# Attention with routed experts on one core: biases loaded as rows, gates and shared product ahead of the keys' second half, the scale product with one tensor from SBUF

## What is computed

```python
q = (x @ Wq + bq).reshape(b, h, t, dh)            # 16 heads of 128; a plain reshape, no transpose
k = (x @ Wk + bk).reshape(b, t, h, dh).transpose(0, 2, 3, 1)
v = (x @ Wv + bv).reshape(b, t, h, dh).transpose(0, 2, 1, 3)
logits = jnp.einsum('bhtd,bhds->bhts', q, k) * scale          # causal mask, softmax
out = jnp.einsum('bhts,bhsd->bhtd', weights, v).transpose(0, 2, 1, 3).reshape(b, t, h * dh) @ Wo + bo
...
shared = jax.nn.silu(g_s) * y_s @ w_shared_down               # g_s, y_s halves of x @ w_shared_up
scores = jax.nn.sigmoid(x_flat @ w_gate)                      # 64 experts, 6 of them for each token
# each expert takes its first 128 tokens: silu(x @ g) * (x @ v) @ w_down, added with normalised scores
```

## Time and profile before

| | |
|---|---|
| median of 3 runs | 1931.96 us (1929.65 to 1937.21) |
| the profiled execution | 1928.67 us |
| its span on the core | 1926.9 us |
| mean granted PE clock | 0.964 of full speed |
| PE busy | 1666.5 us (86%) |
| DVE busy | 1536.8 us (80%) |
| ACT busy | 1083.2 us (56%) |
| POOL busy | 1154.6 us (60%) |
| DMA, mean | 127 GB/s |

### The profile page before, as it was taken

The page is one execution under the profiler, slowest core; times in us unless marked ns, Lnnn a source line. Parts: engine busy times, 40 slices in busy tenths (PEclk is TensorE's granted clock), DMA queues, the critical chain, the costliest instruction groups (busy, mean ns, idle before and its releaser), DMA issues. The chain is left out here.

```text
span 1926.9 us, 49610 instructions
## 1 busy us (share of the span) xinstructions
PE 1666.5 (86%) x19088; PEld 1296.6 (67%) x19088; DVE 1536.8 (80%) x3189; ACT 1083.2 (56%) x2347; POOL 1154.6 (60%) x1004
## 2 busy tenths in 40 slices
PE   1589989999899999999876789998998989999996
PEld 1466777777667777777655767766676776677674
DVE  4888878888788888888854458988988898988885
ACT  0556566666566666656552236655665655566564
POOL 0156667777677777777660027666666666766653
PEclk8799999999999999999997589999999999999999
DMA  9266656565655555545557648777878778777865
GB/s 346 95 136 118 120 114 123 122 114 104 124 90 95 92 99 99 93 87 94 118 95 201 193 112 140 124 133 132 144 129 142 130 143 135 130 123 127 149 119 103
DMA packets 692723, 245.04 MB, mean 127 GB/s; under 512 B 643584, under 2 KB 680785, under 8 KB 691600
## 3 DMA queue, kind: packets, MB, share of 16 engines
q1 hardware_dynamic: 657344, 197.80, 56.1%
q0 software_dynamic: 18432, 33.64, 7.1%
q10 hardware_dynamic: 16720, 10.51, 1.9%
HBM read 57.11 MB, written 50.46 MB: 56 GB/s over the span
## 5 line engine op out<-in xcount | busy, mean ns | idle before, releaser
L476 POOL TENSOR_TENSOR prob<-prob 128x128 f16<-128x128 f32 (+7 forms) x512 | 662.5, 1297 | 626.9 <-ACT prob L856 620.2
L849 ACT ACTIVATE prob<-prob,nmax 128x128 f32<-128x128 f32 (+7 forms) x512 | 397.0, 775 | 644.3 <-DVE prob L1291 631.5
L687 PE MATMUL ps_s<-kT,qT 128*128 128x512 f16 (+3 forms) x2304 | 457.6, 326 | 7.3 <-DVE prob L1291 3.6
L702 PE MATMUL ps_o<-probT,vh 128*128 128x256 f16 (+1 forms) x3840 | 425.3, 264 | 6.5 <-DMA probT<-prob 5.8
L1291 DVE TENSOR_SCALAR_CACHE_REDUCE prob<-ps_s,neg_scale 128x128 f32<-128x128 f32 (+7 forms) x512 | 409.8, 808 | 2.9 <-PE ps_s L689 2.0
L702 PEld LDWEIGHTS ps_o<-probT,vh 128*128 128x128 f16 x3840 | 367.4, 99 | 50.7 <-issue 7.5
L856 ACT CAST prob<-prob 128x128 f16<-128x128 f32 (+7 forms) x512 | 341.5, 667 | 2.2
L687 PEld LDWEIGHTS ps_s<-kT,qT 128*128 128x128 f16 x2304 | 199.5, 98 | 147.0 <-issue 13.1
L716 PE MATMUL ps_y<-wo,oT 128*128 128x256 f16 x1536 | 210.8, 273 | 85.6 <-DVE oT L1306 58.5
L579 PE MATMUL ps_t<-xT,wq 128*128 128x64 f16 x6144 | 202.5, 195 | 61.8 <-DVE z L1193 22.9
L579 PEld LDWEIGHTS ps_t<-xT,wq 128*128 128x128 f16 x6144 | 193.3, 99 | 73.5 <-issue 33.2
(11 more groups left out here) (173 smaller groups left out, 1759.4 us busy)
## 6 DMA issues: line engine op xcount, KB each, us to landing
dispatched<-zeros SPq DMA_DIRECT2D x16, 512.0 KB, 14.8
probT<-prob SPq DMA_TRANSPOSE x512
ex<-dispatched SPq DMA_DIRECT2D x16, 512.0 KB, 4.5
expert_out<-eo ACTq DMA_DIRECT2D x16, 512.0 KB, 4.0
eup<-in_L_ffn_w_up_dram SPq DMA_DIRECT2D x64, 64.0 KB, 2.1
dispatched<-xn,slot_idx POOLq DMA_INDIRECT x192
xn_columns<-xnth SPq DMA_DIRECT2D x24, 128.0 KB
got<-expert_out,slot_idx POOLq DMA_INDIRECT x192
```

Of the source, the lines that this page charges most:

```text
L476: pool.tensor_tensor(low_cols(j), prob_cols(j).rearrange("p (r k) -> p r k", k=P), high_cols(j), ALU.subtract).then_inc(p_low, 1)
L687: pe.matmul(s_cols(j, lo, hi), qT[:, u, a, j * P:(j + 1) * P], kT[:, u, c, lo:hi], start=(n == 0), stop=(n == 2 and hi < w))
L702: mm = pe.matmul(ps_o[:, lo:2 * P], vh[:, u, a, r * D:(r + 1) * D], probT[:, PT_AT[c] + 2 * r + s, lo:], start=(r + n == 0), stop=(r == 2 ...
L849: nc.scalar.activation(prob_cols(j), prob_cols(j), ACT.Exp, bias=nmax[:, j:j + 1], scale=-1.0, accum_out=rsum[:, i % 2, j:j + 1]).then_inc ...
```

## The change

It does three things. (1) The biases are loaded by SP, behind the first batch of x, as 48 rows of 128 into `bias_rows`, which POOL has cleared; PE turns them with one transpose into `ps_o`, and DVE builds `bvB` from there and copies `bqT` and `bkT`. ACT issues no loads at the start. (2) In the heads PE does `gates` and `shared_down` ahead of `project_k(i + 1, 1)`; ACT does `copy_gates` ahead of `high_k(i, 1)`; DVE does `take_logits` and `add_shared` ahead of `low_k(i, 1)`, moves `low_q(i, 1)` behind `block_max(i, 1)`, and `top_indices` and `choose` behind `full_q`; POOL does its three additions for the mask one or two blocks later. (3) `yscale` is computed by a scalar product whose scalar is `out_scale`, with a minimum accumulated into `yleast`, which nothing reads.

```diff
-        bvT = psb("bvT", [P, H])
+        bias_rows = psb("bias_rows", [P, D])
...
             sp.dma_start(resid[:, 0:TB, :], x_v[:, 0:TB, :]).then_inc(x_in[0], 16)
+            sp.wait_ge(bias_zero, 1)
+            for n, b in enumerate((bq, bk, bv)):
+                sp.dma_start(bias_rows[n * H:(n + 1) * H, :], b.rearrange("(m d) -> m d", d=D)).then_inc(bias_in, 16)
...
         def _(pool):
+            pool.memset(bias_rows[:], 0.0).then_inc(bias_zero, 1)
...
-                        if odd_part(i) >= 0 and j in (1, 2, 3):
-                            add_chosen(odd_part(i), j - 1)
+                        if odd_part(i) >= 0 and j == 2:
+                            add_chosen(odd_part(i), 0)
+                        if odd_part(i) >= 0 and j == 3:
+                            add_chosen(odd_part(i), 1)
+                            add_chosen(odd_part(i), 2)
...
             pe.wait_ge(const_ready, 5)
+            pe.wait_ge(bias_in, 48)
+            pe.transpose(ps_o[:, 0:P], bias_rows[:], ident[:]).then_inc(bias_done, 1)
...
                     scores(i, 7)
-                    if more:
-                        project_k(i + 1, 1)
                     if even_part(i) >= 0:
                         gates(i, even_part(i))
                     if odd_part(i) >= 0:
                         shared_down(i, odd_part(i))
+                    if more:
+                        project_k(i + 1, 1)
...
-            act.dma_start(bqT[:], bq.rearrange("(m d) -> d m", d=D)).then_inc(bias_in, 16)
-            act.dma_start(bkT[:], bk.rearrange("(m d) -> d m", d=D)).then_inc(bias_in, 16)
-            act.dma_start(bvT[:], bv.rearrange("(m d) -> d m", d=D)).then_inc(bias_in, 16)
...
-                    high_k(i, 1)
                     if odd_part(i) >= 0:
                         copy_gates(odd_part(i))
+                    high_k(i, 1)
...
-            dve.wait_ge(bias_in, 48)
-            V.tensor_copy(bvB[:], bvT[:].unsqueeze(2).to_broadcast([P, H, P])).then_inc(bias_ready, 1)
+            dve.wait_ge(bias_done, 1)
+            V.tensor_copy(bvB[:], ps_o[:, 2 * H:3 * H].unsqueeze(2).to_broadcast([P, H, P])).then_inc(bias_ready, 1)
+            V.tensor_copy(bqT[:], ps_o[:, 0:H]).then_inc(bias_taken, 1)
+            V.tensor_copy(bkT[:], ps_o[:, H:2 * H]).then_inc(bias_taken, 1)
+            dve.wait_ge(bias_taken, 2)
...
-                V.tensor_tensor(yscale[:], rinv[:], out_scale[:].to_broadcast([P, TB]), ALU.mult).then_inc(r_step, 1)
+                V.tensor_scalar(yscale[:], rinv[:], out_scale[:], None, ALU.mult, ALU.min, accum_out=yleast[:]).then_inc(r_step, 1)
...
                     block_max(i, 0)
-                    low_q(i, 1)
                     mix_at(0)
-                    low_k(i, 1)
                     if odd >= 0:
                         take_logits(odd)
                     if late >= 0:
                         add_shared(late, NC * (i - 1))
+                    low_k(i, 1)
...
                     block_max(i, 1)
+                    low_q(i, 1)
...
-                    if odd >= 0:
-                        top_indices(odd)
-                        choose(odd)
...
                         full_q(i + 1, 1)
+                    if odd >= 0:
+                        top_indices(odd)
+                        choose(odd)
```

More of the change, by code:

```diff
@@ L155, in causal_attention_with_moe @@
         x_in = [sem(f"x_in{n}") for n in range(3)]
+        bias_zero = sem("bias_zero")
         bias_in = sem("bias_in")
+        bias_done = sem("bias_done")
+        bias_taken = sem("bias_taken")
         w_in = sem("w_in")
@@ L264, in causal_attention_with_moe @@
         yscale = sb("yscale", [P, TB])
+        yleast = sb("yleast", [P, 1])
         pro = ExitStack()
```

## The result

The changed kernel takes 1921.8 us in the median (1915.7 to 1923.0, 5 runs) where the kernel before, on the same chip, takes 1933.8 (1929.7 to 1937.2): ratio 0.9931, 95% interval 0.9908 to 0.9955. It is faster, but by a third of what was forecast (1897.0), and it lies above the range (1875 to 1918). The profiled execution of after took 1922.98 us, its span is 1921.2, 5.7 shorter than before's 1926.9.

What follows compares the result with a forecast made beforehand. The DVE and ACT chain was taken as the bound, with PE ahead of it. -19.6 - 30.8 - 1.8 + 14.0 + 4.2 - 0.9 = -34.9 from 1928.67 gave 1893.8, with the runs' median 3.3 higher 1897; range 1875 to 1918.

Steps and rivals of the forecast that it cites:

- the late heads: 27 heads, 35 to 62 without 47: faster `yscale`, less the moved `low_q`, starts `qf` 1.14 us earlier each; -30.8 us.
- the turns: Turns of batch, heads 15, 31, 47: SP's queue behind `prob` 7 sets xT and hides the delay; 0 us.
- the even heads: 16 early heads: `low_q` fits a gap and only holds up the indirect DMA, 0.26 us each; +4.2 us.
- the odd heads: 14 early heads with routing: moved `low_q` is in the chain, block maximum 2 comes 1.0 us later; +14.0 us.
- the start: Before head 0: bias loads leave ACT's queue, square root 10.4 us earlier, `bvB` 21.2 earlier; -19.6 us in all.
- Rival (d): Start gives nothing, as the loads or PE at its half clock hold it: -15.3 us, 1917; chance 0.07.
- the product doesn't wait: Late heads' `yscale`, beside POOL's `prob` 7: 0.27 us against 2.19 before, -1.9 us.
- rival (c): The new product still waits for the rest of POOL's `prob` 7, with `low_q` on top: 1951, slower; chance 0.09.
- two SBUF inputs wait, one does not: DVE beside POOL's product: two-input `yscale` waits, 2.09 us; the reciprocal with one SBUF input takes 0.19.
- PE's waits at nothing: In the heads: DVE and ACT form the chain, PE runs ahead, so each edit is costed by that chain alone.
- (a): The move of `low_q` is absorbed by missed slack, heads 0 to 32 stay: -53.1 us, 1879; chance 0.17.
- (b): PE sets the early heads, so its 44.5 us of waits come back: -97.6 us, 1834; chance 0.05.

Runs made afterwards that it cites:

- filled: The changed kernel plus 24 unread small products on TensorE in every even early head where it waits for the query slices: 1908.7 us, ratio 0.9876.
- reorder_only: The kernel before with the reordering alone, without the bias part and the scale product: 1973.8 us, ratio 1.0204.
- low_q_late: The kernel before with bias part, scale product and, of the reordering, only `low_q`'s second half moved behind block maximum 1: 1918.0 us, ratio 0.9918.
- together: The changed kernel with `low_q`'s second half back, slot indices behind the query slices, and turn loads one transposition earlier: 1839.0 us, ratio 0.9524.

## Why the prediction was right or wrong

Of the 29.2 us between the forecast sum (-34.9) and the measured one (-5.7) the late heads are 18.9, the turns 8.7 and the even heads 8.5; the odd heads came out 6.7 better.

**Right: the start.** -19.6 forecast, -20.4 in the trace, -22.7 (ratio 0.9888) in the run of the part alone. `bvB` was forecast at 21.7 with 2.2 us and stood at 21.23 with 2.28; the table load did go ahead of the wait. Rival (d) fell.

**Right: the product doesn't wait, and rival (c) fell, but for another reason than I gave.** 0.22 us against the 0.27 I took. But the step "two SBUF inputs wait, one does not" is wrong as a rule: the plain form with one SBUF input takes 2.10 us, to the end of POOL's product. The row I leant on, the reciprocal, could not tell the forms apart, and `neg_mean`, which could have, I gave to the rival with 0.09. Had the product been written in the plainer way, (c) would have come true.

**Wrong: the size of the late heads, -30.8 for -11.9.** The mechanism held up to `qf`, which came 0.96 us earlier (forecast 1.14), with the keys waiting 0.75. The step that failed is the next: I let the gain at `qf` stand for the head's. Behind `qf` stands a mixing step, which has two SBUF inputs, and the earlier `qf` moved it onto POOL's indirect DMA: 0.95 us for 0.45. Block maximum 2 came only 0.46 earlier (8.47 us into head 53 for 8.93) and the ordinary late head with it. Mixing behind block maximum 2 brought the head to 24.55 us. Seven heads (40, 41, 48, 54, 55, 61, 62) did gain 0.8 to 1.0; in all seven no indirect DMA was under way when the mixing step started, and it took 0.45 to 0.59 us.

**Wrong by omission: what the move of `low_q` costs.** I priced it into the late heads' sum (1.9 less 0.75) and read it as part of the change; it is where most of the money was. Before, it lay in a gap that exists in every head (the keys wait for ACT), at no cost. In its new place, after against the same kernel with it back, it costs 1.4 us in an ordinary late head (0.9 in the seven), 0.83 in an odd one and 0.48 in an even one. With it back, the change takes 1866.5 us.

**Odd heads, +7.3 for +14.0.** Right in its steps: keys 0.28 later (forecast 0.25), `low_q` 0.93 long and ending 5.9 us into the head. The sum to block maximum 2 is +0.70, not +1.0, since `chosen` and the rest take 0.2 less behind `qf`; heads 5 and 7 lost next to nothing, and head 17 was 0.5 shorter.

**Even heads, +12.7 for +4.2.** The indirect DMA beside `low_q` took 1.25 us instead of 0.99, as forecast, and `picked` came 0.40 later, not 0.26; the other 0.13 is there with `low_q` back in its place too. Head 20 of after, POOL and DVE, answers to the earlier trace rows:

```profile
626.59 1.25 POOL L517 DMA_INDIRECT dispatched<-xn,slot_idx  x1 [0.16 <-issue]
627.87 1.67 POOL L508 TENSOR_TENSOR picked<-chosen,slots_e 128x768 f32<-128x768 bf16 x1
```

```profile
629.57 0.95 DVE L1261 TENSOR_REDUCE i8f<-picked 128x12 f32<-128x768 f32 x1 [2.59 <-POOL picked L508]
```

The other part is the step that cost "PE's waits at nothing". A wait does cost when the granted clock falls after it, by what the run `filled` gave back: 0.23 us in an ordinary even head, 1.2 and 2.0 in heads 6 and 4.

**Turns, +8.7 for 0.** That SP's queue sets xT and hides the rest is half true: the rows' landing sets the turn, and it did not stay where it was. In head 47 PE's wait ended 11.30 us after the head's start before, 13.65 after, though SP issued the loads only 0.43 later; and the same 96 products of the queries took 3.15 us before, at a granted clock of 1.00, and 5.15 after, at 0.53, nearly all of it the lower level. PE in order of time, before and after, and then the stretches of these products, before and after (columns as above):

```profile
1478.73 2.80 PE L579 MATMUL ps_t<-xT,wq 128*128 128x64 f16 x90 [1.42 <-DMA xT<-xn_columns]
1481.75 0.35 PE L579 MATMUL ps_t<-xT,wq 128*128 128x64 f16 x6 [0.22 <-issue]
```

```profile
1480.05 5.15 PE L592 MATMUL ps_t<-xT,wq 128*128 128x64 f16 x96 [5.64 <-DMA xT<-xn_columns]
```

```profile
1478.73:1482.10 3.37, 3.15 (x97) 2.96 (x98) 3.22 (x7) 1.80 (x5) 1.93 (x2) 1.00 0.84 221
```

```profile
1480.05:1485.20 5.15, 5.15 (x97) 5.08 (x98) 1.02 (x1) 0.00 (x0) 1.53 (x2) 0.53 1.17 254
```

The reordering alone doesn't do it: the version without it loses 3.2 us in this head too, and `reorder_only` loses none. It goes with the faster product: head 47 takes 27.3 to 27.7 us in the four kernels whose product doesn't accumulate, and 29.6 to 31.7 in all ten whose product does. PE comes to the wait earlier, the rows don't, and the longer wait is paid in clock. Why they land later is open; issuing them earlier didn't help in this head. Head 52 (+1.7), in which PE waited 2.06 us for `probT`, is open too: `low_q_late` repeats it (27.46 us) and most of the other versions don't, though in the version without the reordering the issue of the same transposition took even longer (4.02 us for 3.94) and the head 24.12.

**Rivals (a) and (b)** fell: the early heads lost 25 us. That PE had 1.76 us of room in odd heads was true, and worth nothing.

## What to carry to other kernels

An instruction that fills a wait is free only where it stands; before moving it, ask what will stand in that wait instead, and follow the chain behind the new place to the next semaphore that another engine waits for, with what shares ports on the way. When a change has three parts, one of them may hide the worth of another: here two parts gave 66 us and the third took 53. And a long wait of TensorE that costs nothing in the chain can still cost in the clock of what it does next.

## What was not expected of the hardware

A `tensor_scalar` of 128x8 that accumulates took 0.21 to 0.22 us in 64 of 64 cases, most of them beside a 2.2 us product of GpSimd; the same without the accumulation took up to 2.10. An unneeded result made it faster. A mixing step (VectorE, 128x256, two SBUF inputs) that started inside a GpSimd product, at least 0.2 us before its end, ended 0.28 to 0.29 us after it, in 98 of 98 cases in after and 71 of 71 in before; beside GpSimd's indirect DMAs the same kind of step was held to their end in some meetings and not in others. A wait of TensorE of 2.3 us for `qf` in head 20 was followed by a stretch at the lower of its two levels, 1.2 GHz (mean 0.94 over a head of 28 us), and one of 1.0 us was not; but one of 2.6 us in head 15 of `together` was not either. And the issue of one transposing DMA on SyncE took from 1.2 to 3.9 us in the heads with nothing changed in it (head 52: 1.83 before, 3.94 after at the same place), which no run here explains.
